# A four-layer kernel in float32: seven feed-forward sums begun in PSUM by VectorE, a new opening, a divided last sum, and the channel mix's sum on VectorE

## The reference

```python
x = x + attn_a(layernorm(x), W_q)          # (xn Wq^T) xn^T xn, no softmax
x = x + ffn(layernorm(x), w1, b1, w2, b2, gamma, beta)
x = x + attn_b(layernorm(x), ...)          # time mix (a scan over tokens) and channel mix
x = x + ffn(layernorm(x), w1, b1, w2, b2, gamma, beta)

def ffn(y):                                # expert 0 alone counts
    z = y + relu(y @ w1 + b1) @ w2 + b2
    return (z - mean(z)) * rsqrt(var(z) + eps) * gamma + beta
def attn_b(x):                             # xa = layernorm with gain; xk, xv, xr mix a token with the one before
    k, v, r = xk @ Wk.T, xv @ Wv.T, xr @ Wr.T
    x = x + (sigmoid(r) * wkv(decay, first, k, v)) @ Wo.T
    kk = square(relu(xk2 @ ffn_Wk.T))      # xc = layernorm of that x
    return x + sigmoid(xr2 @ ffn_Wr.T) * (kk @ ffn_Wv.T)
```

## Time and profile before

| what | us |
|---|---|
| median of 3 runs | 265.02 (264.71 to 265.19) |
| the profiled execution's own time | 266.14 |
| its span, from first to last instruction | 264.3 |
| TensorE busy in the span | 255.3 (97%), 1544 records |
| VectorE busy | 228.2 (86%), 748 |
| ScalarE busy | 227.2 (86%), 440 |
| GpSimd busy | 159.0 (60%), 298 |

### The profile page before, as it was taken

The page is one execution under the profiler, slowest core; times in us unless marked ns, Lnnn a source line. Parts: engine busy times, 40 slices in busy tenths (PEclk is TensorE's granted clock), DMA queues, the critical chain, the costliest instruction groups (busy, mean ns, idle before and its releaser), DMA issues. The chain is left out here.

```text
span 264.3 us, 5318 instructions
## 1 busy us (share of the span) xinstructions
PE 255.3 (97%) x1544; PEld 191.7 (73%) x1544; DVE 228.2 (86%) x748; ACT 227.2 (86%) x440; POOL 159.0 (60%) x298
## 2 busy tenths in 40 slices
PE   7999999999999999999999999999999999999990
PEld 7987886866876686776588658757778658678770
DVE  3498569999999999999999999999999998637443
ACT  1397988999999999999989999999989979895630
POOL 4457676482498179179659827956069637445641
PEclk9999999999999999999999999999999999999996
DMA  6930420203022226303704130622046744725574
GB/s 184 297 110 0 82 42 1 42 15 64 2 42 40 40 42 103 58 2 67 133 2 75 18 67 2 119 41 43 0 71 120 126 85 115 126 43 87 118 150 122
DMA packets 18316, 19.15 MB, mean 72 GB/s; under 512 B 1520, under 2 KB 11632, under 8 KB 18288
## 3 DMA queue, kind: packets, MB, share of 16 engines
q0 software_dynamic: 7056, 12.85, 28.4%
q1 hardware_dynamic: 11232, 5.97, 8.0%
HBM read 3.87 MB, written 2.10 MB: 23 GB/s over the span
## 5 line engine op out<-in xcount | busy, mean ns | idle before, releaser
L1048 PEld LDWEIGHTS bank<-W,f_h 128*128 128x128 f32 x512 | 61.9, 192 | 8.4 <-issue 6.7
L1048 PE MATMUL bank<-W,f_h 128*128 128x128 f32 x512 | 64.3, 275 | 0.0
L1032 PE MATMUL bank<-f_yT,W 128*128 128x512 f32 x128 | 62.3, 598 | 0.0
L821 ACT ACTIVATE f_h<-bank,B1C 128x512 f32<-128x512 f32 x64 | 41.6, 681 | 9.5 <-PE bank L1032 8.2
L1096 PEld LDWEIGHTS bank<-FWv,KK 128*128 128x128 f32 x256 | 31.7, 192 | 5.0 <-issue 3.6
L1096 PE MATMUL bank<-FWv,KK 128*128 128x128 f32 x256 | 33.6, 275 | 0.0
L1032 PEld LDWEIGHTS bank<-f_yT,W 128*128 128x128 f32 x128 | 21.1, 190 | 16.7 <-issue 7.7
L1090 PE MATMUL bank<-XK,FWk 128*128 128x512 f32 x64 | 30.7, 599 | 0.0
L758 ACT ACTIVATE f_y<-R,f_yn_nb,f_yn_rs 128x128 f32<-128x128 f32 x64 | 26.3, 488 | 0.2 <-POOL f_yn_nb L315 0.2
L878 ACT ACTIVATE KK<-bank 128x512 f32<-128x512 f32 x32 | 18.4, 592 | 2.4 <-PE bank L1090 2.3
L882 ACT ACTIVATE KK<-KK 128x512 f32<-128x512 f32 x32 | 19.5, 625 | 0.1
(11 more groups left out here) (144 smaller groups left out, 655.2 us busy)
## 6 DMA issues: line engine op xcount, KB each, us to landing
R<-BETA POOLq DMA_DIRECT2D x16, 256.0 KB, 3.4
R<-f_zg POOLq DMA_DIRECT2D x10, 256.0 KB, 3.4
R<-in_hidden SPq DMA_DIRECT2D x8, 256.0 KB, 3.9
R<-N POOLq DMA_DIRECT2D x8, 256.0 KB, 3.6
out_x<-R SPq DMA_DIRECT2D x8, 256.0 KB, 2.3
R<-G POOLq DMA_DIRECT2D x7, 256.0 KB, 3.5
f_y<-B2R POOLq DMA_DIRECT2D x4, 256.0 KB, 5.7
R<-f_y POOLq DMA_DIRECT2D x4, 256.0 KB, 3.9
```

Of the source, the lines that this page charges most:

```text
L821: a.activation(at(f.h, b)[:, n, :], banks[bank][:], ACT.Relu, bias=B1C[:, n:n + 1]).then_inc(f.h_ready[n], 1)
L1032: t_.matmul(banks[bank][:], W1[:, n * P:(n + 1) * P], at(f.yT, b)[:], start=True, stop=True).then_inc(f.h_psum[n], 1)
L1048: last = t_.matmul(banks[bank][:, j * C:(j + 1) * C], at(f.h, b)[:, n, j * P:(j + 1) * P], W2[:, n, :], start=(n == 0 and j == 0 and b in ...
```

## The change

Batches 0 to 3 of `f1` and 5 to 7 of `f2` (`STARTED`) have their sum z begun in PSUM by VectorE: `ffn_start` of VectorE writes y + B2R into the bank, and the four `ffn_down` add to it. The other nine batches have the transposes of TensorE. `IN_SBUF`, `down_residual`, `z_sum`, `z_sum_stats` and `z_sum_scaled` are gone. In the started batches y is transposed and multiplied without the bias of the second layer. `cmix_out` on VectorE takes the place of `cmix_sum` in all batches. Batch 0 is loaded in two halves, the second by ScalarE's queue, which also loads the vectors, and its first norm goes by halves. `warm_up` is 10 products of a zero tile. The last sum goes into two banks, two rows of tokens in each, and statistics, scale and store go by halves. The hidden tiles `h` have one buffer in place of two, and y three in place of four. The order of the calls is new on all engines.

```diff
-COPIES = {"N": 3, "f1_y": 4, "f2_y": 4, "f1_yT": 2, "f2_yT": 2, "f1_h": 2, "f2_h": 2, "XN": 3, "XNT": 2, "GRAM": 2,
-          "PROJ": 2, "f1_zg": 3, "f2_zg": 3, "others": 1}
-ADDED = {"f1": (0,), "f2": (7,), "x3": (7,)}
+COPIES = {"N": 3, "f1_y": 3, "f2_y": 3, "f1_yT": 2, "f2_yT": 2, "XN": 3, "XNT": 2, "GRAM": 2, "PROJ": 2,
+          "f1_zg": 3, "f2_zg": 3, "others": 1}
+ADDED = {"f1": (0,), "f2": (7,), "x3": tuple(range(BATCHES))}
-IN_SBUF = {"f2": (1, 3, 5, 6)}
+STARTED = {"f1": (0, 1, 2, 3), "f2": (5, 6, 7)}
+FIRST, LAST = ((0, 1), (2, 3)), ((0, 1), (2, 3))
...
+            def ffn_start(b, f, bank, *free):
+
+                if b == f.started[0]:
+                    dve.wait_ge(*b2_rows.done(0, "centred"))
+                for s, count in free:
+                    dve.wait_ge(s, count)
+                dve.wait_ge(*f.norm.ready.done(b, "all"))
+                v.tensor_tensor(bank_rows(bank), at(f.y, b)[:], B2R[:].unsqueeze(1).broadcast_to([P, J, C]), ALU.add).then_inc(f.y_psum, 1)
...
+            act.dma_start(R[0][:, FIRST[1][0]:, :], hidden.rearrange("b (j p) c -> b p j c", p=P)[0][:, FIRST[1][0]:, :]).then_inc(x0_loaded[0], DMA)
+            act.dma_start(VEC[:], vectors).then_inc(vec_loaded, DMA)
...
+            def last_down_first(n, *pair):
+
+                pe.wait_ge(f2.y_psum, len(f2.started) + len(LAST) - 1)
+                pe.wait_ge(f2.h_ready[n], B)
+                for rows, bank in zip(LAST, pair):
+                    for j in rows:
+                        t_.matmul(banks[bank][:, j * C:(j + 1) * C], at(f2.h, B - 1)[:, n, j * P:(j + 1) * P], W2[:, n, :], start=False,
+                                  stop=False, skip_group_check=True)
...
             def warm_up(bank, count):
 
+                pe.wait_ge(*warm.done(0, "tile"))
                 for _ in range(count):
-                    t_.transpose(banks[bank][:, 0:P], IDENT[:], IDENT[:])
...
+                    last = t_.matmul(banks[bank][:, 0:P], WROW[:, 0:P], WROW[:, 0:P], start=True, stop=True)
```

More of the change, by code:

```diff
@@ new lines, in last_out @@
+            def last_out(part):
+                dve.wait_ge(*last[part].done(0, "rs"))
+                dve.wait_ge(f2.zg_ready, B + part)
+                dve.wait_ge(*f2.xb.ready(B - 1))
+                for j in LAST[part]:
+                    done = v.scalar_tensor_tensor(R[B - 1][:, j, :], at(f2.zg, B - 1)[:, j, :], f2.znorm.rs[(B - 1) % 2][:, j:j + 1],
+                                                  R[B - 1][:, j, :], ALU.mult, ALU.add)
+                done.then_inc(last[part].sem(0), 1)
@@ L458, in mean_var @@
                     dve.wait_ge(*(back.done(b - 2, "back") if n is nt else n.scale.done(b - 2, "rs")))
+                if n is na and b == 2:
+                    dve.wait_ge(*first.done(0, "rs"))
+                    dve.wait_ge(*na.ready.done(0, "all"))
                 for j in range(J):
@@ new lines, in last_start, with warm_tile @@
+            def last_start(part, bank, *free):
+                for s, count in free:
+                    dve.wait_ge(s, count)
+                dve.wait_ge(*f2.norm.ready.done(B - 1, "all"))
+                c = slice(LAST[part][0], LAST[part][-1] + 1)
+                v.tensor_tensor(bank_rows(bank)[:, c, :], at(f2.y, B - 1)[:, c, :], B2R[:].unsqueeze(1).broadcast_to([P, len(LAST[part]), C]),
+                                ALU.add).then_inc(f2.y_psum, 1)
+            def warm_tile():
+                v.memset(WROW[:], 0.0).then_inc(warm.sem(0), 1)
@@ L744, in _ @@
[L744 to L746 removed]
+                dve.wait_ge(vec_loaded, DMA)
+                dve.wait_ge(*decay.done(0, "rate"))
+                dve.wait_ge(*warm.done(0, "psum"))
+                v.tensor_scalar(WROW[:], WROW[:], WDEC[:], None, ALU.add).then_inc(decay.sem(0), 1)
@@ new lines, in _ @@
+            bias_part(5, gate.done(0, "rl")); ffn_down(3, f1, 1, 4); hidden_up(4, f1, 1, 2); product_o(0, 1)
+            ffn_down(3, f1, 2, 4); ffn_down(3, f1, 3, 4); hidden_up(4, f1, 0, 1, (u1_ready, 1))
+            product_v(1, 5, (b1_ready, 1)); attn_gram(7, 3, x1.ready(6)); hidden_up(4, f1, 2, 2, (f1.h_ready[1], 5))
+            ffn_start(4, f1, 1, (f1.h_ready[0], 5)); product_r(1, 7); tmix_transpose(2, 0); hidden_up(4, f1, 3, 6)
+            ffn_down(4, f1, 0, 1); ffn_down(4, f1, 1, 1); ffn_transpose(5, f1, 6, (f1.h_ready[3], 5))
@@ new lines, in _ @@
+            hidden_up(6, f1, 0, 6, (f1.h_ready[2], 7)); cmix_down(0, 2, 7); product_k(3, 2)
+            ffn_start(6, f1, 1, cgate.done(0, "rl")); cmix_transpose(1, 5, (f1.h_ready[3], 7))
+            product_v(3, 3, gate.done(2, "rl")); ffn_down(6, f1, 0, 1); product_o(2, 5, (xc_ready, 2))
+            tmix_transpose(4, 2, expo.done(3, "diff")); cmix_down(0, 3, 7); product_r(3, 5); cmix_up(1, 0, 0)
+            ffn_transpose(7, f1, 7, cgate.done(0, "kvs")); cmix_up(1, 1, 6); ffn_down(6, f1, 1, 1)
@@ new lines, in _ @@
+            ffn_down(2, f2, 2, 3); cmix_down(4, 3, 6); ffn_down(2, f2, 3, 3); product_k(7, 0); cmix_up(5, 0, 2)
+            ffn_transpose(3, f2, 7, gate.done(6, "rl")); cmix_up(5, 1, 4); cmix_up(5, 2, 2, square[0].done(5, "relu"))
+            product_o(6, 7, (f2.yT_ready, 4)); hidden_up(3, f2, 0, 4, square[1].done(5, "relu"))
+            cmix_up(5, 3, 2, square[2].done(5, "relu")); hidden_up(3, f2, 1, 0, expo.done(7, "diff"))
+            ffn_start(3, f2, 4, (f2.h_ready[0], 4)); hidden_up(3, f2, 2, 7, (u1_ready, 7))
```

772 lines of the change are left out of this document (394 added, 378 removed).

## The result

| | before | changed |
|---|---|---|
| median | 265.65 us (6 runs beside it) | 268.54 us (6 runs), 267.94 us (9 more, in a second series) |
| time to before | | ratio 1.0106 [1.0066, 1.0146], second series 1.0068 [1.0044, 1.0092] |
| profiled execution: own time, span | 266.14, 264.3 | 268.02, 266.2 |

The changed kernel is slower by 0.7 to 1.1%. The forecast was 265.1, in a range of 262.5 to 267.5: wrong in size, and no change was forecast where there is a loss.

What follows compares the result with a forecast made beforehand. A relay: VectorE sets the pace up to `product_o(7)`, then TensorE's remaining work, then the tail. TensorE ends at 258.9; 258.9 + 2.4 + 3.1 = 264.4 us span, 265.1 as median; range 262.5 to 267.5.

Steps and rivals of the forecast that it cites:

- Opening: From the start to `z_stats(1, f1)`: first product at 6.8 us, `z_stats(1, f1)` at 35.5, 4.8 us earlier than before.
- the rival, with 0.13: Opening: TensorE's clock is low after the short warm-up, first products slow, +2.4 us, 267.5 in all; chance 0.13.
- VectorE sets the pace up to `product_o(7)`: From `z_stats(1, f1)` to `gated(7)`: VectorE's operations, net +1.5 us, set the time; 180.0 us taken, `product_o(7)` at 215.7.
- the rival of dear new operations: Long stretch: six new VectorE operations at 0.73 us and idle time kept, 267.1; sign: stretch over 180.5 us; chance 0.15.
- VectorE was idle for 1.4 us of the stretch: From `z_stats(1, f1)` to `gated(7)`: VectorE's idle time should shrink as inputs are ready; range 179.8 to 181.2, taken 180.0.
- the upper end that the prediction gave: Highest length forecast for the stretch from `z_stats(1, f1)` to `gated(7)`: 181.2 us.
- Behind `product_o(7)` 43.2 us for TensorE: After `product_o(7)` TensorE's remaining work sets the time: 37.1 + 6.1 = 43.2 us, ending at 258.9.
- Tail: Behind TensorE's end: 2.4 us for the half's statistics, power and sum, 3.1 for the store, 5.5 in all.
- Removed DMAs and the single h at nothing: Removed adding DMAs cost nothing, as GpSimd has slack and they ended in time; `relu` waiting for single `h` costs nothing.
- The profiled execution's own time was 266.14, 1.1 above the median of the runs; the difference goes to the median.: Step from the forecast span of 264.4 us to the median: 265.1, using the profiled execution's 1.1 us above the median.

Runs made afterwards that it cites:

- run 5: The changed kernel again, unchanged, on one chip with the later runs: 267.94 us; eight of nine between 267.7 and 268.2, one at 269.62.
- run 2: Changed kernel with the second and third quarter of the channel mix's second product left out for batches 0 to 4: 271.13 us.
- run 13: Run 11's kernel with the second and third quarter of the channel mix's second product left out for batches 0 to 4: 266.92 us.
- run 14: Run 11's kernel with four more VectorE operations of 128x512 into an unread tile, behind gated(1) to gated(4): 268.98 us.
- run 6: Changed kernel with three moves in the orders of GpSimd and ScalarE, no operation added or removed: 266.80 us, ratio to before 1.0036.
- run 12: Run 6's kernel with the second and third quarter of the channel mix's second product left out for batches 6 and 7: 266.51 us.
- run 7: Kernel before with only the last feed-forward sum divided into two halves, with statistics, power, sum and store by halves: 264.53 us, ratio 0.9951.
- run 9: Run 6's kernel with the channel mix's sums of batches 0 to 3 by an adding DMA again: 266.29 us.
- run 10: Run 6's kernel with two buffers in place of one for the hidden tile h of both feed-forward networks: 266.79 us.
- run 4: Kernel before with the channel mix's sums of batches 0 to 3 by VectorE in place of the adding DMA: 270.85 us, ratio 1.0160.
- run 3: Changed kernel with one move on GpSimd, bias(3, f2.norm) ahead of back_shift(7): 269.36 us.
- run 8: Kernel before with the divided last sum and the new opening (first batch by halves, 20 warm-up transposes in place of 44): 263.90 us, ratio 0.9924.
- run 11: Run 6's kernel with 13 warm-up products in place of 10: 266.71 us.
- run 15: Run 8's kernel with 26 warm-up transposes in place of 20: 263.29 us, ratio 0.9904 to the kernel before.

## Why the prediction was wrong

Its steps, one by one, by the sum that it made against the profiled executions:

- *Opening*, 4.8 us earlier: 5.1. Right. The power over 128x2 is 0.71 and 0.82 us (0.6 taken). The first product ran at the upper level here and at the lower in the profiles of runs 5 and 2; the rival, with 0.13, had about the frequency of run 5, one in nine, and cost 1.5 us, not 2.4.
- *VectorE sets the pace up to `product_o(7)`*: right, and shown by runs 13 and 14. Its work grew by 1.0 us where the count said 1.5. So the rival of dear new operations is not borne out, though its sign, a stretch of more than 180.5 us, came: the operations cost the 0.60 us that were taken (2.4 us for four in run 14), and it was idle time that made the stretch long.
- *"VectorE was idle for 1.4 us of the stretch, mostly at its start, waiting for others; being later relative to TensorE now, it should find its inputs ready."* This step failed. The idle time went to 3.17 us, and the stretch to 182.43 in place of 180.0. The listed waits (1.4, 0.7 and 0.3 us) were not for TensorE, but for ScalarE, and behind the longest of them ScalarE waited for GpSimd. I had read from GpSimd's busy share (113.9 of 179.7) that it had slack; but in an in-order queue it is the time to the one awaited result that counts, and here a power of 1.98 us and two operations of another norm stood ahead of it. 1.2 us of the 2.4 that were missed come back with three moves (run 6); the other 1.2 are an idle time of 1.97 where I wrote 0.2, less 0.6 of work that I had too much. The stretch of run 6, 181.20, is the upper end that the prediction gave. What lies behind the other two waits was not followed.
- *Behind `product_o(7)` 43.2 us for TensorE*: 43.08. The size is right, the reason only half of it: run 12 shows a second chain of the same length, so taking work off TensorE there would have won nothing.
- *Tail*, 5.5: 5.4. Right in the changed kernel. On before alone it is 6.4 (run 7), because of the store, of which the prediction said that it keeps 3.1: it took 2.8 in the one and 3.7 in the other.
- *Removed DMAs and the single h at nothing*: right in size (runs 9 and 10), within 0.5 us. But the DMAs did not simply end before they were needed: with four of them back VectorE waits 1.3 us for their landing.
- *"The profiled execution's own time was 266.14, 1.1 above the median of the runs; the difference goes to the median."* This failed too, for another 1.1 us. The median of 265.02 came from three executions; in the larger groups beside the later runs (11 to 35 executions) the kernel before has medians from 265.8 to 266.4, and 266.14 lies among them. Nor is such a difference a constant. In the profiled execution of before the first 24 warm-up transposes took 5.38 us; in that of run 7, with the same opening, they took 4.25, and the first product came at 8.34 in place of 9.50, in an execution of 264.24 us:

```profile
6.12 2.38 PE L1188 MATMUL bank<-IDENT 128*128 128x128 f32 x20
8.34 1.06 PE L1056 MATMUL bank<-XN 128*128 128x128 f32 x8
```

The kernel before pays for a late rise of the clock with a longer warm-up, 44 transposes whatever happens. The changed one waits for `XN0` and not for its warm-up, so it had nothing of this to give back. The Trainium skill, page "TensorE: Matmul & The Clock Gate", section "Part 1: The HAM clock gate", says that one kernel shows different numbers of cold matmuls from run to run; the rows of the same 24 transposes, in three kernels with one opening (5.38, 4.99 in run 4, 4.25), agree.

So 264.4 became 266.2 (1.8, of it 2.4 in the stretch less 0.3 in the opening and 0.3 of roundings and small terms), and the way from the profile to the median was -1.1 in the forecast, and near 0 in the second series, +0.5 in the first. Against the kernel before, the sum is 5.1 won in the opening and 1.6 in the tail, 2.7 lost in the stretch and 6.0 behind it, because the new order leaves that much more work behind `product_o(7)`: 1.9 slower by the spans.

## What to carry to other kernels

Where one engine is full, ask of each in-order queue beside it what stands behind the operation that waits, and for how long its one awaited result is under way, not how busy that engine is on average: GpSimd had 40% to spare, and its late scale cost 1.4 us. A profiled execution that is above the median may be so for a reason that the change removes, or because the median is of three executions; find the row that holds the difference before it is carried over. And test a pace by adding work to the engine that is thought to set it: four idle operations told in one run what removing work, with its new waits and a clock that fell, had not told in three.

## What was unexpected of the hardware

- A power of GpSimd over 128x4 values took 1.0 us alone, and mostly so beside VectorE (median 1.03 of 43). One of them, beside an unbroken VectorE, took 2.22 or 2.23 us in eleven executions and 4.00 in one.
- TensorE's clock fell to its lower level after an idle time of 1.9 us (run 3, 0.57 over the four microseconds that follow) and of 2.0 us (run 2, 0.79 over eight that begin with the idle time), and so less work for TensorE made a kernel slower. Behind a short warm-up and 1.2 us of idleness it was still at the lower level in run 5; after the same warm-up and 1.02 us it was at the upper one in the changed kernel. With a warm-up that ended 0.23 to 0.65 us before the first product no execution stood 1 us or more above its median (runs 11, 13, 14 and 15, 36 executions); with a gap of 1.1 to 1.3 us three of twelve did in run 6 and three of ten in run 8. That these had the slow first product is not shown, since none of them was profiled.
- An adding DMA of 256 KB landed after 3.3 us in one execution (run 7) and 4.7 in another (run 8) at the same place of the program.
